# Projections of the next sample in two visits per slot in place of four, in an attention kernel between two expert layers

## The chip, the cores and the metric

The kernel runs on one core of a Trainium2 chip. The metric is device time in microseconds for one execution, from the median of several runs. TensorE multiplies matrices, VectorE reduces and combines, ScalarE evaluates exponentials and copies, GpSimd does masks and part of the rotary embedding, SyncE issues the DMAs. All of them run side by side and meet at semaphores.

## The reference, cut to what matters

Three layers follow one another on an input of 32 samples of 512 tokens and 256 features: an expert layer, attention with 16 heads of 16 features, and the expert layer again. The change is in the attention layer.

```python
x = x + 0.5 * ffn(layernorm(x))          # two experts of eight, chosen per sample
qkv = layernorm(x) @ Wqkv.T              # 512 x 768 for each sample
q, k = rotate(q), rotate(k)              # rotary embedding
attn = softmax(causal(q @ k.T / 4))      # 16 heads, 512 x 512
x = x + (attn @ v) @ Wo.T
x = x + 0.5 * ffn(layernorm(x))
```

## The kernel before

Each layer is a phase of its own. The attention phase (`attention_phase`) goes through the samples in slots: four slots (g = 0 to 3) to a sample, and each slot handles four heads. The work of one sample is spread over several samples' slots. In a slot for group G (sample s, part g) TensorE does, step by step for n = 0 to 10, the maxima scores of group G (`max_scores`, L882 to L906), which VectorE reduces to row maxima (L750), and the transposed scores of group G - 2 (`scores`, L908 to L926), on which ScalarE takes the exponential (L817). Scores have two PSUM banks, so step c waits for the exponential c - 2 (L914). Maxima scores have three banks, and a step waits for the reduction that last used its bank (L889). The two use opposite halves of TensorE's rows. Steps 0 to 3 have one score matmul of 512 columns, 4 to 7 two of 384 and 128, 8 and 9 two of 256.

Other work of TensorE is put between the steps by hand, in `slot` (L1017 to L1049):
- `turn_maxima` (L879) at n = 1 transposes the maxima of group G - 1. It waits for all eleven reductions of that group.
- `probs_v` (L941) at n = 2 and n = 8 multiplies exponentials with V.
- `turn_output` (L988) at n = 5 transposes the output of group G - 3. It waits for ScalarE's copy of it (L847), which ScalarE does after exponential 3.
- `project_qk` (L956) and `project_v` (L968) project the next sample, s + 1: in g = 0 and 1 two of the four 128-row blocks of Q and K in each slot, in g = 2 the four blocks of V. A block of Q or K is six matmuls of 512 columns, three for each half of the 256 features; a block of V is six matmuls of 256 columns. They use all of TensorE's rows. VectorE takes Q and K from PSUM (`begin_rope`, L724 and L725) behind its reductions 2 and 6, and ScalarE takes V (L864) behind exponentials 4 and 7.
- in g = 3, the transposes of sample s + 2 and the output projection of sample s - 1 (L980, L1002, L1011).

TensorE runs its matmuls in the order of the program. VectorE in g = 1 also has the low parts of rotated Q (`rope_low`, L731), and in g = 2 the layernorm statistics of sample s + 2 (L99 to L111) behind reduction 1. ScalarE copies the high parts of rotated Q and K (L823) in g = 1 and 2.

For the last sample there is no next one, so its slots have no projections. The first slots of the phase have projections but no scores yet.

Of the kernel before, what the change touches and what calls it, by code (L numbers as in the profile page):

```python
# [54 lines left out]
def wait(eng, sem, value):  # L55

    if isinstance(value, int) and value <= 0:
        return
    eng.wait_ge(sem, value)
# [441 lines left out]
def attention_phase(nc, tab, src, dst, cos, sin):  # L501
# [10 lines left out]
    with ExitStack() as ctx:  # L512
# [64 lines left out]
        def group(G):  # L577
            return not isinstance(G, int) or 0 <= G < B * 4

        def sample(s):  # L580
            return not isinstance(s.b, int) or 0 <= s.b < B
# [289 lines left out]
        def _(pe):  # L871
            def part(t, p):
                return t.hi if p == "hi" else t.lo

            def turn_maxima(s, g):

                G = 4 * s.b + g
                pe.wait_ge(max_done, 11 * G)
                nc.tensor.transpose(mx_ps[TURN_BANK][0:NT * GH, 0:P], mx[(g - 1) % 2][:].rearrange("p a i -> p (a i)"),  # L879
                                    tab.ident[:]).then_inc(mt_done, 1)  # L880

            def max_scores(s, g, n):  # L882

                G = 4 * s.b + g

                if n == 4:
                    wait(pe, mt_copied, G)
                else:
                    wait(pe, max_done, 11 * G + (-2, -1, 1, 2, None, 3, 4, 5, 6, 7, 8)[n])  # L889
                if n == 0:  # L890
                    pe.wait_ge(q_stacked, 96 * (s.b + 1))
                    pe.wait_ge(k_stacked, 96 * (s.b + 1))
                bank = mx_ps[MX_BANK[n]]
                i, heads = (3, [n]) if n < 4 else (2, [n - 4]) if n < 8 else (1, [2 * n - 16, 2 * n - 15]) if n < 10 else (0, range(4))
                w, nh = (i + 1) * P, len(heads)
                half, j = half_of(g)
                rows, const = slice(HP * half, HP * half + TERMS_ROWS), slice(HP * half, HP * half + HP)
                for at, a in enumerate(heads):
                    nc.tensor.matmul(bank[:, at * w:at * w + w], q_stack[s.par][rows, j + a, i * P:(i + 1) * P],  # L899
                                     k_stack[s.par][rows, j + a, 0:w], start=(at == 0), stop=False)  # L900

                last = bank[:, 0:nh * w].rearrange("p (a n) -> p a n", a=nh)[:, :, i * P:w]
                over = tab.mask[const, :].rearrange("p (a n) -> p a n", a=1)
                nc.tensor.matmul(last, tab.turn[const, HP:3 * HP], over.broadcast_to([HP, nh, P]), start=False, stop=False)  # L904
                nc.tensor.matmul(last[:, :, HP:P], tab.turn[const, 0:P], over[:, :, 0:HP].broadcast_to([HP, nh, HP]),  # L905
                                 start=False, stop=True).then_inc(mx_done, 1)  # L906

            def scores(s, g, c):  # L908

                G = 4 * s.b + g - 2  # L910
                ss, sg = of_group(s, g, 2)
                bank = st_ps[c % 2]

                wait(pe, exp_done, 10 * G + c - 1)  # L914
                if c == 0:
                    pe.wait_ge(rows_set[g % 2], 16 * (2 * s.b + (g - 2) // 2 + 1))
                a = c % 4 if c < 8 else 2 * (c - 8)
                half, j = half_of(sg)
                rows = slice(HP * half, HP * half + TERMS_ROWS + 1)

                work = [(a, 0, 0, 0)] if c < 4 else [(a, 1, P, 0), (a, 3, 3 * P, 3 * P)] if c < 8 else \
                    [(a, 2, 2 * P, 0), (a + 1, 2, 2 * P, 2 * P)]
                for ha, kt, q0, col in work:
                    ins = nc.tensor.matmul(bank[:, col:col + T - q0], k_stack[ss.par][rows, j + ha, kt * P:(kt + 1) * P],  # L924
                                           q_stack[ss.par][rows, j + ha, q0:T], start=True, stop=True)
                ins.then_inc(st_done, 1)  # L926

            def probs_v(s, g, lag, nth, kt):

                G = 4 * s.b + g - lag  # L930
                ss, sg = of_group(s, g, lag)
                if kt == 0:

                    wait(pe, on_done, G)
                    pe.wait_ge(v_copied, 2 * (ss.b + 1))
                pe.wait_ge(exp_done, 10 * G + (4, 8, 10, 8)[kt])
                pe.wait_ge(masked, 4 * G + nth + 1)
                for a in range(GH):
                    p = (probs[:, a, :], probs[:, 4 + a, 0:3 * P], probs[:, 8 + a // 2, (a % 2) * 2 * P:(a % 2) * 2 * P + 2 * P],
                         probs[:, 4 + a, 3 * P:])[kt]  # L940
                    ins = nc.tensor.matmul(pv_ps[32 * a:32 * a + 32, kt * P:T], v[ss.par][:, kt, head_of(sg, a), :], p,  # L941
                                           start=(kt == 0), stop=(nth == 3), tile_position=(0, 32 * a))
                ins.then_inc(pv_done, 1)

            def project_qk(n, t, half):

                idx = 4 * n.b + t
                if t == 0 and not half:
                    pe.wait_ge(xT_lo, NC * (n.b + 1))
                if t < 2 and not half:  # L950

                    wait(pe, res_done, 2 * (n.b - 2) - 1 + t)
                if t >= 2 and not half:
                    pe.wait_ge(rope_in, idx - 1)
                for i, (wp, xp) in enumerate(TERMS):
                    ins = nc.tensor.matmul(x_ps[t % 2][:], part(tab.qkv, wp)[:, int(half), t * P:(t + 1) * P],  # L956
                                           part(xT, xp)[:, int(half), :], start=(i == 0 and not half), stop=(i == 2 and half))
                if half:
                    ins.then_inc(qk_done, 1)

            def project_v(n, t):

                if t % 2 == 0:
                    pe.wait_ge(rope_in, 4 * (n.b + 1) - 1 + t // 2)
                i = 0
                for c in range(NC):
                    for xp, wp in TERMS:
                        ins = nc.tensor.matmul(x_ps[t // 2][:, (t % 2) * D:(t % 2) * D + D], part(xT, xp)[:, c, t * P:(t + 1) * P],  # L968
                                               part(tab.qkv, wp)[:, c, 2 * D:3 * D], start=(i == 0), stop=(i == 3 * NC - 1))
                        i += 1  # L970
                if t % 2:
                    ins.then_inc(v_done, 1)
# [44 lines left out]
            def slot(s, g):  # L1017
                G = 4 * s.b + g
                cur, run = group(G), group(G - 2)
                if isinstance(G, int) and G == 0:  # L1020
                    pe.wait_ge(stacks_set, 64)
                before = group(G - 3)
                for n in range(11):
                    if run and n < 10:
                        scores(s, g, n)
                    if cur:
                        max_scores(s, g, n)
                    if n == 2 and before:
                        probs_v(s, g, 3, 1, 1)
                    if n == 1 and group(G - 1):  # L1030
                        turn_maxima(s, g)
                    if n == 2 and before:
                        probs_v(s, g, 3, 2, 3)
                        probs_v(s, g, 3, 3, 2)
                    if n == 5 and before:
                        turn_output(s, g)
                    if g < 2 and sample(s + 1) and n in (0, 1, 4, 5):
                        project_qk(s + 1, 2 * g + (n > 3), half=(n in (1, 5)))
                    if g == 2 and sample(s + 1) and n in (0, 1, 4, 5):
                        project_v(s + 1, (0, 1, 4, 5).index(n))  # L1040
                    if g == 3 and sample(s + 2) and n == 0:
                        transposes(s + 2)
                    if run and n == 8:
                        probs_v(s, g, 2, 0, 0)
                    if g == 3 and sample(s + -1) and n == 4:
                        transpose_o(s + -1, s)
                    if g == 3 and sample(s + -1) and n >= 9:
                        project_o(s + -1, 2 * (n - 9))
                        project_o(s + -1, 2 * (n - 9) + 1)  # L1049

            schedule(pe, slot)


# [57 lines left out]
```

## Time and profile before

| | |
|---|---|
| median of 3 runs | 2402.93 us (2398.98 to 2409.86) |
| profiled execution | 2401.97 us |
| its span in the trace | 2400.2 us |
| matmuls busy | 2190.0 us (91%) |
| weight loads busy | 1279.8 us (53%) |
| VectorE busy | 1956.3 us (82%) |
| ScalarE busy | 1357.7 us (57%) |
| GpSimd busy | 1280.2 us (53%) |
| granted TensorE clock, mean | 0.979 |

The attention phase takes from about 440 to 2000 us of the span. In the timeline a row has the start, the duration, the engine, the line, the operation with output and inputs, and in brackets the idle time of the engine before it with who released it. "PE" is TensorE's matmuls and "PEld" its weight loads. Matmuls overlap one another in the rows, since each is shown until its result has landed: the pitch from start to start is what it costs in a stream.

### The profile page before, as it was taken

To read this page: it belongs to the slowest core of one execution; us is meant where nothing else is said; L and a number is where in the kernel's file an instruction comes from. 1 tells how busy PE (TensorE), PEld (TensorE's weight loads), DVE (VectorE), ACT (ScalarE), POOL (GpSimd) and SP (SyncE) were. 2 spreads that over 40 slices of the span, in tenths; PEclk is the share of its full clock that TensorE was granted. 3 is DMA by queue.
4 is the path that set the end of the run, shared out by engine and by line. 5 is a ranking of instruction groups with operands and counts; after the bars stand their busy time and mean duration, and the time that the engine had idled before them with its cause. 6 is when DMAs were issued, how large, how long until landed. Compare 5 with 4: busy or idle time off the path is not lost. (4 is left out here: it accounts for less than half of the span.)

```text
span 2400.2 us, 56572 instructions
## 1 busy us (share of the span) xinstructions
PE 2190.0 (91%) x19596; PEld 1279.8 (53%) x19596; DVE 1956.3 (82%) x4345; ACT 1357.7 (57%) x2567; POOL 1280.2 (53%) x1458
## 2 busy tenths in 40 slices
PE   2999999399999999999999999999999986999999
PEld 1666666245554555555455455545545543666666
DVE  4777777379989989998998999899899864777776
ACT  2455545046666666666666666666666663455454
POOL 3666666335545544554554555455455424666664
PEclk9999999779999999999999999999999997999999
DMA  5566665323444444344344434444433513665664
GB/s 162 172 203 204 203 204 191 88 63 89 97 89 93 95 92 90 89 99 89 93 95 89 90 90 99 89 96 94 86 90 92 93 39 111 187 210 193 208 205 164
DMA packets 280284, 295.50 MB, mean 123 GB/s; under 512 B 45664, under 2 KB 263104, under 8 KB 280000
## 3 DMA queue, kind: packets, MB, share of 16 engines
q1 hardware_dynamic: 279456, 290.83, 46.8%
q8 instruction: 157, 2.57, 0.5%
q14 instruction: 127, 1.04, 0.2%
q10 hardware_dynamic: 544, 1.05, 0.1%
HBM read 140.08 MB, written 83.89 MB: 93 GB/s over the span
## 5 line engine op out<-in xcount | busy, mean ns | idle before, releaser
L817 ACT ACTIVATE at_probs<-at_st_ps 128x512 f32<-128x512 f32 x1280 | 748.2, 604 | 508.6 <-PE at_st_ps L924 499.1
L750 DVE TENSOR_REDUCE at_mx<-at_mx_ps 128x1 f32<-128x512 f32 (+3 forms) x1408 | 839.8, 634 | 141.3 <-PE at_mx_ps L905 139.6
L672 POOL TENSOR_SCALAR_AFFINE_SELECT at_probs<-at_probs 128x512 f32<-128x512 f32 x512 | 320.5, 639 | 710.6 <-ACT at_probs L817 710.6
L899 PE MATMUL at_mx_ps<-at_k_stack,at_q_stack 48*128 48x512 f16 (+3 forms) x2048 | 502.3, 303 | 20.7 <-DVE at_mx L750 10.7
L924 PE MATMUL at_st_ps<-at_q_stack,at_k_stack 49*128 49x512 f16 (+3 forms) x2048 | 459.5, 302 | 65.7 <-ACT at_probs L817 64.2
L428 ACT ACTIVATE f_h<-f_h_ps,f_b1s 128x512 f32<-128x512 f32 x256 | 176.0, 688 | 359.2 <-PE f_h_ps L470 347.7
L924 PEld LDWEIGHTS at_st_ps<-at_q_stack,at_k_stack 49*128 49x128 f16 x2048 | 135.8, 94 | 433.4 <-ACT at_probs L817 332.0
L904 PE MATMUL at_mx_ps<-mask,turn 64*128 64x128 bf16 (+2 forms) x1408 | 342.2, 243 | 0.0
L941 PE MATMUL at_pv_ps<-at_probs,at_v 128*32 128x512 f32 (+3 forms) x4096 | 331.4, 441 | 0.3 <-POOL at_probs L672 0.3
L905 PE MATMUL at_mx_ps<-mask,turn 64*128 64x64 bf16 (+2 forms) x1408 | 281.5, 200 | 0.0
L486 PE MATMUL f_y_ps<-f_w2hi,f_hlo 128*128 128x256 f16 x1024 | 279.1, 273 | 0.0
L486 PE MATMUL f_y_ps<-f_w2hi,f_hhi 128*128 128x256 f16 x1024 | 279.1, 273 | 0.0
L486 PE MATMUL f_y_ps<-f_w2lo,f_hhi 128*128 128x256 f16 x1024 | 279.1, 273 | 0.0
L470 PE MATMUL f_h_ps<-f_xThi,f_w1hi 128*128 128x512 f16 x512 | 198.0, 387 | 30.1 <-DVE f_xTlo L377 29.8
L99 DVE BATCH_NORM_STATS2 f_stats<-f_x 128x6 f32<-128x256 f32 x256 | 89.8, 413 | 144.1 <-DMA f_x<-after_attention 72.7
L470 PE MATMUL f_h_ps<-f_xThi,f_w1lo 128*128 128x512 f16 x512 | 197.4, 385 | 0.0
L470 PE MATMUL f_h_ps<-f_xTlo,f_w1hi 128*128 128x512 f16 x512 | 196.9, 385 | 0.0
L678 POOL TENSOR_TENSOR at_by_sin<-at_swapped,at_sin 128x512 f32<-128x512 f32 x128 | 175.2, 1369 | 35.2 <-DVE at_swapped L725 35.2
L682 POOL TENSOR_TENSOR at_rotated<-at_by_cos,at_by_sin 128x512 f32<-128x512 f32 x128 | 182.1, 1423 | 18.8
L386 DVE TENSOR_TENSOR f_hlo<-f_h,f_hhi 128x512 f16<-128x512 f32 x256 | 173.2, 733 | 20.1 <-ACT f_hhi L429 20.1
L337 POOL TENSOR_TENSOR f_res<-f_x,f_b2q 128x1024 f32<-128x1024 f32 x64 | 151.1, 2361 | 61.5 <-DMA after_ffn<-f_res 30.6
L899 PEld LDWEIGHTS at_mx_ps<-at_k_stack,at_q_stack 48*128 48x128 f16 x2048 | 154.7, 93 | 54.2 <-DVE at_mx L750 25.6
(118 smaller groups left out, 4240.0 us busy)
## 6 DMA issues: line engine op xcount, KB each, us to landing
at_q_stack<-qk_image SPq DMA_DIRECT2D x192, 128.0 KB, 4.3
at_k_stack<-qk_image SPq DMA_DIRECT2D x192, 128.0 KB, 4.4
f_x<-in_x SPq DMA_DIRECT2D x32, 512.0 KB, 5.6
f_w1hi<-w_hi SPq DMA_DIRECT2D x128, 128.0 KB, 2.3
f_w1lo<-w_lo SPq DMA_DIRECT2D x128, 128.0 KB, 2.1
f_b2s<-in_b SPq DMA_DIRECT2D x128, 128.0 KB, 3.7
f_w2hi<-w_hi SPq DMA_DIRECT2D x128, 128.0 KB, 4.2
f_w2lo<-w_lo SPq DMA_DIRECT2D x128, 128.0 KB, 4.2
```

Of the source, the lines that this page charges most:

```text
L428: nc.scalar.activation(h32[j][:], h_ps[j][:], ACT.Gelu, bias=bias).then_inc(gelu_done, 1)
L470: ins = nc.tensor.matmul(h_ps[j][:], w, v, start=(n == 0), stop=(n == 3 * NC - 1))
L486: ins = nc.tensor.matmul(y_ps[t // 2][:, t % 2, :], v, w, start=(n == 0), stop=(n == 11))
L672: nc.gpsimd.affine_select(out=ap, in_=ap, compare_op=ALU.is_ge, fill=0.0, base=0, pattern=[[0, d] for d in dims] + [[1, P]], channel_multi ...
L682: nc.gpsimd.tensor_tensor(rotated[t % 2][:], by_cos[t % 2][:], by_sin[t % 2][:], ALU.add).then_inc(rope_done, 1)
L750: nc.vector.tensor_reduce(o_ap, i_ap, AX_X, ALU.max).then_inc(max_done, 1)
L817: nc.scalar.activation(probs[:, c, :], st_ps[c % 2][:], ACT.Exp, scale=DH ** -0.5).then_inc(exp_done, 1)
L899: nc.tensor.matmul(bank[:, at * w:at * w + w], q_stack[s.par][rows, j + a, i * P:(i + 1) * P], k_stack[s.par][rows, j + a, 0:w], start=(at ...
L904: nc.tensor.matmul(last, tab.turn[const, HP:3 * HP], over.broadcast_to([HP, nh, P]), start=False, stop=False)
L905: nc.tensor.matmul(last[:, :, HP:P], tab.turn[const, 0:P], over[:, :, 0:HP].broadcast_to([HP, nh, HP]), start=False, stop=True).then_inc(m ...
L924: ins = nc.tensor.matmul(bank[:, col:col + T - q0], k_stack[ss.par][rows, j + ha, kt * P:(kt + 1) * P], q_stack[ss.par][rows, j + ha, q0:T ...
L941: ins = nc.tensor.matmul(pv_ps[32 * a:32 * a + 32, kt * P:T], v[ss.par][:, kt, head_of(sg, a), :], p, start=(kt == 0), stop=(nth == 3), ti ...
```

## The change

In slots g = 0 and 1, the first half of a block of Q or K ran behind step 0 and its second half behind step 1; the next block's halves ran behind steps 4 and 5. Now both halves run behind step 1, and both of the next behind step 5. In slot g = 2, the four blocks of V ran behind steps 0, 1, 4 and 5; now two run behind step 1 and two behind step 5. The matmuls, their operands and their waits stay as they are.

```diff
-                    if g < 2 and sample(s + 1) and n in (0, 1, 4, 5):
-                        project_qk(s + 1, 2 * g + (n > 3), half=(n in (1, 5)))
-                    if g == 2 and sample(s + 1) and n in (0, 1, 4, 5):
-                        project_v(s + 1, (0, 1, 4, 5).index(n))
+                    if g < 2 and sample(s + 1) and n in (1, 5):
+                        project_qk(s + 1, 2 * g + (n > 3), half=False)
+                        project_qk(s + 1, 2 * g + (n > 3), half=True)
+                    if g == 2 and sample(s + 1) and n in (1, 5):
+                        project_v(s + 1, 2 * (n > 3))
+                        project_v(s + 1, 2 * (n > 3) + 1)
```

## Rows read from the trace of the kernel before

**Rows 1.** Busy time by stretches, one sample: engines, granted clock, DMA share, GB/s.
```profile
core 0: us, PE busy (x) PEld busy (x) DVE busy (x) ACT busy (x) POOL busy (x), PEclk, DMA share, GB/s
1000.00:1046.60 46.60, 44.37 (x453) 23.76 (x452) 42.28 (x98) 30.25 (x61) 24.15 (x30) 1.00 0.40 92
```

**Rows 2.** Waits of TensorE, 480 to 1960 us: total, times, longest.
```profile
PE at_st_ps L924 <- ACT at_probs L817: 61.0, 129, 0.6
```

**Rows 3.** Timeline of TensorE, a slot g = 0 of a middle sample.
```profile
1180.93 0.39 PE L924 MATMUL at_st_ps<-at_q_stack,at_k_stack 49*128 49x512 f16 x1
...
1182.50 0.28 PE L879 MATMUL at_mx_ps<-ident,at_mx 128*16 128x128 f32 x1
1182.62 0.38 PE L956 MATMUL at_x_ps<-at_xThi,qkv_hi 128*128 128x512 f16 x1
1182.83 0.38 PE L956 MATMUL at_x_ps<-at_xThi,qkv_lo 128*128 128x512 f16 x1
...
1183.36 0.39 PE L924 MATMUL at_st_ps<-at_q_stack,at_k_stack 49*128 49x512 f16 x1
...
1185.20 0.39 PE L924 MATMUL at_st_ps<-at_q_stack,at_k_stack 49*128 49x512 f16 x1
...
1186.97 0.66 PE L988 MATMUL at_pv_ps<-ident,at_o 128*128 128x128 f32 x4
1187.46 0.38 PE L956 MATMUL at_x_ps<-at_xThi,qkv_hi 128*128 128x512 f16 x1
...
1188.21 0.33 PE L924 MATMUL at_st_ps<-at_q_stack,at_k_stack 49*128 49x384 f16 x1
...
1190.84 0.28 PE L924 MATMUL at_st_ps<-at_q_stack,at_k_stack 49*128 49x256 f16 x1
...
1191.24 0.33 PE L899 MATMUL at_mx_ps<-at_k_stack,at_q_stack 48*128 48x128 f16 x3
1191.36 0.39 PE L924 MATMUL at_st_ps<-at_q_stack,at_k_stack 49*128 49x512 f16 x1
```

**Rows 4.** Timeline, slot g = 0 of the last sample, without projections: TensorE, then ScalarE's copy.
```profile
1925.77 0.39 PE L924 MATMUL at_st_ps<-at_q_stack,at_k_stack 49*128 49x512 f16 x1
...
1926.48 0.28 PE L879 MATMUL at_mx_ps<-ident,at_mx 128*16 128x128 f32 x1
...
1928.87 0.39 PE L924 MATMUL at_st_ps<-at_q_stack,at_k_stack 49*128 49x512 f16 x1
...
1930.00 0.33 PE L924 MATMUL at_st_ps<-at_q_stack,at_k_stack 49*128 49x384 f16 x1 [0.41 <-ACT at_probs L817]
...
1930.49 0.66 PE L988 MATMUL at_pv_ps<-ident,at_o 128*128 128x128 f32 x4
...
1929.84 0.59 ACT L847 ACTIVATE at_o<-at_pv_ps 128x512 f32<-128x512 f32 x1
```

**Rows 5.** Timeline of VectorE and TensorE, slots g = 1 and 2 of the middle sample.
```profile
1191.45 1.28 DVE L750 TENSOR_REDUCE at_mx<-at_mx_ps 128x2 f32<-128x512 f32 x2
...
1201.68 0.28 PE L924 MATMUL at_st_ps<-at_q_stack,at_k_stack 49*128 49x256 f16 x1
...
1202.51 0.39 PE L899 MATMUL at_mx_ps<-at_k_stack,at_q_stack 48*128 48x128 f16 x4 [0.26 <-DVE at_mx L750]
...
1203.07 0.38 PE L924 MATMUL at_st_ps<-at_q_stack,at_k_stack 49*128 49x512 f16 x1
...
1203.57 1.27 DVE L750 TENSOR_REDUCE at_mx<-at_mx_ps 128x4 f32<-128x512 f32 x2
...
1208.17 0.68 DVE L750 TENSOR_REDUCE at_mx<-at_mx_ps 128x1 f32<-128x512 f32 x1
1208.91 0.33 PE L899 MATMUL at_mx_ps<-at_k_stack,at_q_stack 48*128 48x384 f16 x1
...
1210.50 0.33 PE L924 MATMUL at_st_ps<-at_q_stack,at_k_stack 49*128 49x384 f16 x1
```

**Rows 6.** Timeline of VectorE, the same subtraction in slots g = 1 and 2.
```profile
1193.25 1.25 DVE L731 TENSOR_TENSOR at_qk_lo<-at_rotated,at_qk_hi 128x512 f16<-128x512 f32 x1
...
1204.77 0.68 DVE L731 TENSOR_TENSOR at_qk_lo<-at_rotated,at_qk_hi 128x512 f16<-128x512 f32 x1
```

## The prediction, made before the changed kernel was built or run

> **What bounds the kernel now.** I read the busy shares first, then the waits of TensorE, and then one slot of four heads step by step in the timeline. The view by stretches says that in one sample of the attention phase (46.6 us, four slots) the matmul row is busy 44.37 us, VectorE 42.28, ScalarE 30.25, at a granted clock of 1.00, the 2.4 GHz level [rows 1]. That makes TensorE look full. The weight loads on the same engine are busy 23.76 us, about half. The Trainium skill ("Perfetto Trace Analysis", section "Identifying the Most-Contended Engine") says that the share of matmul busy time isn't a measure of how close TensorE is to its limit, since matmuls are pipelined, and points to the share of weight loads. These rows agree that 95% and 51% describe the same stretch.
>
> The waits show who holds TensorE up: between 480 and 1960 us the score matmuls (L924) wait for ScalarE's exponentials 129 times, 61.0 us together [rows 2]. So a slot is a chain in which TensorE and ScalarE take turns: step n+2 of the scores can't start before exponential n is done, since there are two score banks. What one more or one less matmul costs depends on where in this chain it stands. TensorE runs its matmuls in program order, so whatever stands behind a waiting score matmul waits too.
>
> The timeline of a slot g = 0 of a middle sample [rows 3] has its score steps 0, 2, 3, 6 and 9 at 1180.93, 1183.36, 1185.20, 1188.21 and 1190.84, and the next slot at 1191.36: 10.43 us. The best view is one that the kernel gives for free: in the last sample there is no next sample to project, and the same slot g = 0 runs without any projection [rows 4]. It shows what the chain does where the projection is not there to fill it. Its step 3 starts at 1928.87 and step 5 at 1930.00, which is 1.13 us later, held by the exponential of step 3 (the row says 0.41 us idle, released by ScalarE). Its transposes of the output (L988) start at 1930.49, 1.62 us after step 3, behind ScalarE's copy of the output, which ends at 1929.84 + 0.59 = 1930.43.
>
> **The change, part by part.** No matmul is added or taken away. In each slot with g = 0, 1 or 2, half of the first projection goes from step 0 to step 1, and half of the second from step 4 to step 5. The number of visits (a run of full-array matmuls between score steps) falls from four to two per slot.
>
> Unit costs. A visit of three L956 matmuls takes 0.74 us from its first matmul to the next score step (1182.62 to 1183.36) [rows 3], 0.75 after the output transposes (1187.46 to 1188.21). The pitch in it is 0.21 to 0.22 us (1182.62 to 1182.83), so three more matmuls add 0.65, and a visit of six takes 1.40. Six L968 matmuls have half the columns each; I take the same 0.65 for them.
>
> First visit, g = 0. Without projection, step 0 to the transpose of the maxima (L879) is 0.71 us (1925.77 to 1926.48) [rows 4]; from that to the projection 0.12 (1182.50 to 1182.62) [rows 3]. Then step 2 starts at 0.71 + 0.12 + 1.40 = 2.23 after step 0, against 2.43 now. Gain 0.20: that is what a change from half-array to full-array work and back costs, and it is real wherever nothing else is waited for. The Trainium skill ("TensorE: Matmul & The Clock Gate", section "LDWEIGHTS (loading the stationary operand)") gives the 128 columns of a weight load 107 ns; two of them left uncovered per visit would be 0.21, an estimate by that page; the 0.20 of the rows agrees.
>
> Second visit, g = 0. Now the half at step 4 lies in the time in which step 5 would wait for exponential 3. Taken away, step 5 waits: it starts 1.13 after step 3, the transposes of the output 1.62 after it (not 1.77 as now, 1185.20 to 1186.97), the projection 0.49 later (1186.97 to 1187.46), step 6 a further 1.40: 1.62 + 0.49 + 1.40 = 3.51 us, against 3.01 now (1185.20 to 1188.21). Loss 0.50. Behind step 6 nothing has slack: steps 7 and 8 wait for exponentials that follow step 6. So the slot g = 0 becomes 0.30 longer. Bounds for this part: if step 5 had no wait, the gain would be 0.20 again; if the wait hid nothing, the loss is the 0.65 of the three matmuls. I take 0.50, since both ends of it stand in [rows 4].
>
> Slot g = 1. Here the transpose of the maxima has to wait: VectorE ends the last reduction of the slot before at 1191.45 + 1.28 = 1192.73 [rows 5], 1.37 after the slot's start, while now the transpose comes at 1.99 and doesn't feel it. Moved up, it starts at about 1.43; then 0.12 + 1.40 gives step 2 at 2.95 against 2.84 now: loss 0.11 in place of the gain, because six matmuls now stand behind a wait that three of them used to fill. The second visit costs 0.50 again. Of the 0.61 a part is given back: the last maxima step waits for VectorE now. Step 9 at 1201.68 and last maxima matmul at 1202.51 are 0.83 apart (0.26 idle, released by L750), against 0.40 in g = 0 (1190.84 to 1191.24) [rows 3, 5]. VectorE's work in this slot is as before, so these 0.43 are slack for TensorE: 0.61 - 0.43 = 0.18 longer.
>
> Slot g = 2. VectorE's last reduction of g = 1 (1203.57, 0.68 for one) ends 1.18 after the slot's start now [rows 5], and 1.00 after it once the slot starts 0.18 later, so the transpose of the maxima starts at 1.06; + 0.12 + 1.40 = 2.58 for step 2. Now it is 2.48: loss 0.10. In the second visit the maxima of step 5 start at 1208.91, right when VectorE's reduction of step 2 is done (1208.17 + 0.68 = 1208.85), and that is behind the layernorm statistics, not behind TensorE. It stays where it is, at 5.84. All of the six V matmuls that stood before it now come behind it: 0.65 longer, with step 6 at 8.08 in place of 7.43 (1210.50 - 1203.07), and this includes the 0.10. Slot g = 3 has no projection and keeps its length.
>
> Sum: 0.30 + 0.18 + 0.65 = 1.13 us per sample. Projections run beside scores in the slots of 30 samples, and in one more only in g = 2: 30 x 1.13 + 0.65 = 34.6 us. The profiled execution took 2401.97 us (its span 2400.20 and 1.77 around it), 0.04% below the median of 2402.93. So 2402 + 34.6 gives 2437, which I leave as it is for the median.
>
> What is passed on the way costs nothing: the second half of each projection stays in its place in the order, so the vector engine's rotation, the V copies on ScalarE, GpSimd's products and the SyncE loads and stores behind them are released after the same matmul as before, only later by what step 2 and step 6 are late. The rotation of g = 1 could feel this first. Its cover is VectorE's own queue, which is without a gap in that slot.
>
> **The rivals.**
> A, TensorE is full, and only the switches count. Each visit removed saves 0.20, six per sample: 6 x 0.20 x 31 = 37 us less, 2366. For it speaks the 95% of [rows 1]. Against it stands that step 5 without the half before it waits 0.41 us in [rows 4]. The Trainium skill ("TensorE: Matmul & The Clock Gate", section "Loop structure matters more than you think") asks for matmuls back to back, and by that rule this change is a gain, though none by the clock, which is at 1.00 in [rows 1] already. Chance 0.07.
> B, the delay is swallowed in g = 1 and g = 2, since VectorE is busy 42.28 of 46.6 us and sets their length: then only the 0.30 of g = 0 is left, 30 x 0.30 = 9 us, 2411, not measurable against before. For it speaks the wait at 1202.51; against it that this wait holds only 0.43 and that g = 2 has no such wait at its end. It would need a slack of 0.65 there. Chance 0.13.
> C, the shift also brings VectorE and GpSimd over one another. The same subtraction (L731) takes 1.25 us at 1193.25 and 0.68 at 1204.77 [rows 6]; GpSimd is at work on the rotation beside the first. One more such overlap per sample on the chain of g = 1 costs up to 0.57 x 31 = 18 us: 2455. Chance 0.14.
> The forecast has 0.66.
>
> **How the numbers follow.** Likeliest 2437. Its own bounds are the first visit's 0.11 and 0.10 falling away (30 x 0.2 = 6 less) and the loss of the second at its full 0.65 in g = 0 and 1 (30 x 0.30 = 9 more): 2428 to 2447. The range must hold 8 in 10: forecast and C, up to 2456, and down to 2416, which leaves out A and most of B. A measurement of this kernel can tell about 0.5% (12 us) from no change. Faster by more: A, 0.07. Within: B, 0.13. Slower by more: 0.80.
>
> **What would show it.** In the profile after, in a middle sample: slots of about 10.7, 11.9, 11.2 and 13.9 us; step 2 of g = 0 at 2.23; score step 5 idle 0.4 us or so before it, released by ScalarE, in each of the three slots; waits of L924 for L817 grown by 90 cases or more; in g = 1 the transpose of the maxima released by VectorE, and no wait left before the last maxima step. If step 5 starts less than 1.13 us after step 3, the second visit is wrong; if step 6 in g = 2 is at 7.4, the third term is; if the reductions or L731 are longer than before, C has come.

## The result, and the profile after

The changed kernel takes 2442.86 us (median of 4 executions, 2438.85 to 2449.67), the kernel before 2404.89 us in the same comparison. The ratio is 1.0162, with a 95% interval of 1.0127 to 1.0197: slower by 38 us (31 to 47). The forecast was 2437, a loss of 34.6, in a range of 2416 to 2456.

The view by stretches, for one middle sample, as in [rows 1] (columns as there: engines with busy time and count, granted clock, DMA share, GB/s):

```profile
1197.67:1245.70 48.03, 44.35 (x454) 24.34 (x454) 42.79 (x97) 29.90 (x60) 24.09 (x29) 1.00 0.43 90
```

The sample takes 48.03 us in place of 46.6. The matmuls are busy 44.35 us as before (44.37 in [rows 1]), at the same granted clock. So all of the loss is time in which no matmul is in flight. The waits of TensorE between 480 and 2000 us show the releaser:

```profile
PE at_st_ps L924 <- ACT at_probs L817: 98.9, 221, 0.6
PE at_mx_ps L899 <- DVE at_mx L750: 4.7, 8, 1.4
```

The second row reads in the kernel before, between 480 and 1960 us:

```profile
PE at_mx_ps L899 <- DVE at_mx L750: 10.7, 33, 1.4
```

The score matmuls wait for exponentials 221 times in place of 129 (98.9 us in place of 61.0, [rows 2]): 92 waits more, in 90 or so slots that have both projections and scores. The waits of the maxima matmuls (L899) for VectorE fall from 33 to 8: the one before the last maxima step of g = 1 is gone in nearly every sample.

The timeline of a slot g = 0 answers to [rows 3]:

```profile
1197.67 0.39 PE L924 MATMUL at_st_ps<-at_q_stack,at_k_stack 49*128 49x512 f16 x1
1197.90 0.38 PE L924 MATMUL at_st_ps<-at_q_stack,at_k_stack 49*128 49x512 f16 x1
1198.39 0.28 PE L879 MATMUL at_mx_ps<-ident,at_mx 128*16 128x128 f32 x1
1198.50 0.38 PE L956 MATMUL at_x_ps<-at_xThi,qkv_hi 128*128 128x512 f16 x1
...
1199.89 0.39 PE L924 MATMUL at_st_ps<-at_q_stack,at_k_stack 49*128 49x512 f16 x1
1201.73 0.39 PE L924 MATMUL at_st_ps<-at_q_stack,at_k_stack 49*128 49x512 f16 x1
...
1202.87 0.33 PE L924 MATMUL at_st_ps<-at_q_stack,at_k_stack 49*128 49x384 f16 x1 [0.41 <-ACT at_probs L817]
...
1203.36 0.66 PE L988 MATMUL at_pv_ps<-ident,at_o 128*128 128x128 f32 x4
1203.85 0.38 PE L956 MATMUL at_x_ps<-at_xThi,qkv_hi 128*128 128x512 f16 x1
...
1205.24 0.33 PE L924 MATMUL at_st_ps<-at_q_stack,at_k_stack 49*128 49x384 f16 x1
...
1208.39 0.39 PE L924 MATMUL at_st_ps<-at_q_stack,at_k_stack 49*128 49x512 f16 x1
```

Step 1 now follows step 0 after 0.23 us, and step 2 comes at 2.22 (1199.89 - 1197.67), 0.21 earlier than before. Then step 5 stands 0.41 us for ScalarE, 1.14 behind step 3, and step 6 comes 3.51 behind step 3 (1205.24 - 1201.73) in place of 3.01. The row of step 5 in the last sample of the kernel before [rows 4] had the same 0.41. The same 0.41 stands before step 5 in g = 1 and g = 2.

The slots, each as the median distance between the first score matmuls of neighbouring slots over the middle samples. In one kernel nearly all of them repeat to some hundredths of a microsecond from sample to sample, which is far finer than the times themselves, so the experiments below are read by them:

| us | g = 0 | g = 1 | g = 2 | g = 3 | sum |
|---|---|---|---|---|---|
| before | 10.43 | 11.71 | 10.59 | 13.85 | 46.58 |
| forecast for after | 10.73 | 11.89 | 11.24 | 13.85 | 47.7 |
| after | 10.72 | 11.87 | 11.58 | 13.85 | 48.02 |

Thirty samples at 1.44, and one more g = 2 at 0.99, are 44 us. The spans differ by 42.3 (2442.5 and 2400.2), and the medians by 38. Single executions of one kernel differ by some us. A part of that is the start of the phase: the first score matmul stands at 506.09 in the profiled execution before and at 501.83 in the one after.

### The profile page after: what moved, and what is told of

Read it like the earlier page. It is cut to its first block and busy times, and to the rows that moved or that the text cites. A ratio compares the mean times of both kernels' runs of the same rounds, so it can differ in the third digit from the quotient of the medians.

```text
span 2442.5 us, 56572 instructions
## 1 busy us (share of the span) xinstructions
PE 2190.0 (90%) x19596; PEld 1297.0 (53%) x19596; DVE 1970.9 (81%) x4345; ACT 1347.9 (55%) x2567; POOL 1277.9 (52%) x1458
## 3 DMA queue, kind: packets, MB, share of 16 engines
q1 hardware_dynamic: 279456, 290.83, 46.6%
## 5 line engine op out<-in xcount | busy, mean ns | idle before, releaser
L924 PE MATMUL at_st_ps<-at_q_stack,at_k_stack 49*128 49x512 f16 (+3 forms) x2048 | 450.0, 302 | 102.6 <-ACT at_probs L817 101.4
L899 PE MATMUL at_mx_ps<-at_k_stack,at_q_stack 48*128 48x512 f16 (+3 forms) x2048 | 498.0, 302 | 18.4 <-DMA at_k_stack<-qk_image 10.4
L899 PEld LDWEIGHTS at_mx_ps<-at_k_stack,at_q_stack 48*128 48x128 f16 x2048 | 155.4, 93 | 59.8 <-DVE at_mx L750 27.9
```

## The experiments

**1. Each visit by itself.** The first visit merged, and the second as before:

```diff
-                    if g < 2 and sample(s + 1) and n in (0, 1, 4, 5):
+                    if g < 2 and sample(s + 1) and n in (1, 4, 5):
+                        if n == 1:
+                            project_qk(s + 1, 2 * g, half=False)
                         project_qk(s + 1, 2 * g + (n > 3), half=(n in (1, 5)))
-                    if g == 2 and sample(s + 1) and n in (0, 1, 4, 5):
+                    if g == 2 and sample(s + 1) and n in (1, 4, 5):
+                        if n == 1:
+                            project_v(s + 1, 0)
                         project_v(s + 1, (0, 1, 4, 5).index(n))
```

> Only the first visit is merged (behind step 1); the second stays at steps 4 and 5. Theory T (TensorE's chain, with the exponential of step 3 as the thing the second visit used to hide): g = 0 shorter by 0.20 us (10.23), g = 1 unchanged, since its delay of 0.10 behind the transpose of the maxima is taken by the wait of the last maxima step for VectorE (11.70), g = 2 longer by about 0.18 (10.77), because the transpose of the maxima waits for VectorE until about 1.24 after the slot's start. Sum about 0 per sample: the same time as before, within 3 us. Rival A (switches cost, nothing waits): 0.20 less in each of three slots, 19 us faster than before. Rival M (merging as such is what costs, in either place): about half of the 38 us, some 19 us slower.

Measured: ratio to before 0.9984 (0.9968 to 0.9999), 2398.77 us against 2403.80. Slots 10.22, 11.79, 10.77, 13.85, sum 46.63. Theory T holds in g = 0 (10.23 expected) and g = 2 (10.77); g = 1 is 0.09 longer than expected. The wait that was to take the delay is there, with the same 0.26 us idle as in [rows 5]:

```profile
1200.57 0.40 PE L899 MATMUL at_mx_ps<-at_k_stack,at_q_stack 48*128 48x128 f16 x4 [0.26 <-DVE at_mx L750]
```

It ends later, since VectorE's own queue in g = 1 is longer. VectorE has a second subtraction L731 there, behind reduction 3. It took 1.03 us in the kernel before, and takes 1.12 here, where GpSimd's mask comes later against the slot. In the kernel before:

```profile
1197.44 1.03 DVE L731 TENSOR_TENSOR at_qk_lo<-at_rotated,at_qk_hi 128x512 f16<-128x512 f32 x1
1197.30 0.64 POOL L672 TENSOR_SCALAR_AFFINE_SELECT at_probs<-at_probs 128x512 f32<-128x512 f32 x1 [1.66 <-ACT at_probs L817]
```

In this one:

```profile
1195.42 1.12 DVE L731 TENSOR_TENSOR at_qk_lo<-at_rotated,at_qk_hi 128x512 f16<-128x512 f32 x1
1195.36 0.63 POOL L672 TENSOR_SCALAR_AFFINE_SELECT at_probs<-at_probs 128x512 f32<-128x512 f32 x1 [1.75 <-ACT at_probs L817]
```

Against the slot's start (1191.36 and 1189.34) the mask begins at 5.94 and 6.02, and in both kernels L731 ends 0.53 to 0.55 after it.

Neither A (19 us faster) nor M (19 slower) is borne out. The first visit saves 0.21 where nothing is waited for, and gives it back in g = 1 and 2. The median is 5 us lower all the same, which the slots (0.05 more per sample) don't explain. The executions of this kernel had a mean granted clock of 0.977 to 0.983, all but two of the kernel before 0.974 to 0.977, and the one of those at 0.983 took 2391.76 us. So a few microseconds between medians are no reading of the slots; where in the program they arise was not followed.

The second visit merged, and the first as before:

```diff
-                    if g < 2 and sample(s + 1) and n in (0, 1, 4, 5):
+                    if g < 2 and sample(s + 1) and n in (0, 1, 5):
+                        if n == 5:
+                            project_qk(s + 1, 2 * g + 1, half=False)
                         project_qk(s + 1, 2 * g + (n > 3), half=(n in (1, 5)))
-                    if g == 2 and sample(s + 1) and n in (0, 1, 4, 5):
+                    if g == 2 and sample(s + 1) and n in (0, 1, 5):
+                        if n == 5:
+                            project_v(s + 1, 2)
                         project_v(s + 1, (0, 1, 4, 5).index(n))
```

> Only the second visit is merged (behind step 5); the first stays at steps 0 and 1. Theory T: g = 0 longer by 0.50 us (10.93), g = 1 by 0.07 (11.77, the rest taken by the wait for VectorE), g = 2 by 0.65. If in g = 2 GpSimd's product again slides over VectorE's subtraction L731 (as it does in the changed kernel, where it takes 1.08 us in place of 0.68), g = 2 is longer by 0.99 in all (11.58). Sum 1.2 without and 1.56 with that overlap: 37 or 47 us slower than before, so at least the whole loss of the change. Rival A: 19 us faster. Rival M: about 19 us slower.

Measured: 1.0184 (1.0144 to 1.0223), 2444.43 us. Slots 10.93, 11.78, 11.58, 13.85, sum 48.13: the expected 10.93, 11.77 and 11.58. Of these the 11.58 is no forecast, since its overlap of VectorE and GpSimd was read from the changed kernel, which had run by then. TensorE in g = 0:

```profile
1203.28 0.39 PE L924 MATMUL at_st_ps<-at_q_stack,at_k_stack 49*128 49x512 f16 x1
...
1204.41 0.33 PE L924 MATMUL at_st_ps<-at_q_stack,at_k_stack 49*128 49x384 f16 x1 [0.41 <-ACT at_probs L817]
...
1204.90 0.66 PE L988 MATMUL at_pv_ps<-ident,at_o 128*128 128x128 f32 x4
1205.39 0.38 PE L956 MATMUL at_x_ps<-at_xThi,qkv_hi 128*128 128x512 f16 x1
...
1206.78 0.33 PE L924 MATMUL at_st_ps<-at_q_stack,at_k_stack 49*128 49x384 f16 x1
```

Step 5 waits 0.41 us, and step 6 is 3.50 behind step 3. The second visit alone brings the whole loss.

**2. Is it the number of visits, or the place?** Two visits, but the second one behind step 4, where the exponential is waited for:

```diff
-                    if g < 2 and sample(s + 1) and n in (1, 5):
+                    if g < 2 and sample(s + 1) and n in (1, 4):
...
-                    if g == 2 and sample(s + 1) and n in (1, 5):
+                    if g == 2 and sample(s + 1) and n in (1, 4):
```

> Two visits per slot as in the change, but the second behind step 4 in place of step 5: all six matmuls lie in the time in which step 5 would wait for exponential 3. Theory T taken on TensorE alone: step 3 to step 6 takes 3.00 us in place of 3.51, g = 0 is 10.22, and the kernel is 40 us or so faster than the changed one and within 8 us of before. Theory T with VectorE's queue: the output transposes come 0.64 later behind step 3 than before, VectorE's normalisation with them, and its reduction 6 in g = 0 starts 0.4 us later; since VectorE has no gap from there to the end of g = 1, the last maxima step of g = 1 waits longer and g = 1 grows by up to 0.6: 10 to 20 us slower than before, still 20 to 30 faster than the changed kernel. Rival M (two visits are worse than four wherever they stand): as slow as the changed kernel, 38 us slower than before.

Measured: 1.0044 (1.0029 to 1.0058), 2415.42 us. Slots 10.50, 11.88, 10.77, 13.85, sum 47.00. Seven tenths of the loss per sample are gone (0.42 in place of 1.44), so rival M falls: with the same two visits it is the place that counts. The kernel stays 12 us slower than before, where the version of the theory with VectorE's queue had 10 to 20. Step 3 to step 6 is 3.01 us, as expected:

```profile
1187.84 0.39 PE L924 MATMUL at_st_ps<-at_q_stack,at_k_stack 49*128 49x512 f16 x1
...
1189.90 0.33 PE L924 MATMUL at_st_ps<-at_q_stack,at_k_stack 49*128 49x384 f16 x1
...
1190.26 0.66 PE L988 MATMUL at_pv_ps<-ident,at_o 128*128 128x128 f32 x4
...
1190.85 0.33 PE L924 MATMUL at_st_ps<-at_q_stack,at_k_stack 49*128 49x384 f16 x1
```

The version of the theory with TensorE alone falls too. The output transposes come 2.42 behind step 3, and VectorE's queue is late with them. VectorE in this kernel, in the same slot:

```profile
1190.38 0.56 DVE L750 TENSOR_REDUCE at_mx<-at_mx_ps 128x1 f32<-128x384 f32 x1 [0.87 <-PE at_mx_ps L905]
1190.95 0.26 DVE L762 RECIPROCAL at_inverse<-at_pv_ps 128x16 f32<-128x16 f32 x1
1191.31 0.62 DVE L767 TENSOR_TENSOR at_on<-at_pv_ps,at_inverse 128x64 f32<-128x64 f32 x4
1191.85 0.55 DVE L750 TENSOR_REDUCE at_mx<-at_mx_ps 128x1 f32<-128x384 f32 x1
```

It stands idle 0.87 us ahead of reduction 5, and reduction 6 comes 1.00 after step 6 (1191.85 - 1190.85). In the kernel before it comes 0.47 after step 6, which stands at 1188.21 [rows 3]:

```profile
1188.68 0.56 DVE L750 TENSOR_REDUCE at_mx<-at_mx_ps 128x1 f32<-128x384 f32 x1
```

From there VectorE has no gap. The last maxima step feels it, and already in g = 0: it stands 0.68 behind step 9 (1194.15 and 1193.47), where it stood 0.40 behind it before, so the slot is 10.50 and not 10.22. I had expected the wait in g = 1 alone. There it shows at the transpose of the maxima, which starts 1.66 after the slot's start (1195.94 - 1194.28).

**3. The transpose of the maxima.** The changed kernel, with this transpose behind the first projection:

```diff
-                    if n == 1 and group(G - 1):
-                        turn_maxima(s, g)
...
                         project_v(s + 1, 2 * (n > 3) + 1)
+                    if n == 1 and group(G - 1):
+                        turn_maxima(s, g)
```

> The changed kernel, with the transpose of the maxima behind the first projection of the slot in place of ahead of it. If in g = 1 the six matmuls stand idle behind its wait for VectorE (it starts 1.43 after the slot's start), they now start at about 1.25, step 2 comes at 2.76 in place of 2.94, and g = 1 shrinks from 11.87 to 11.69. In g = 2 step 2 comes 0.2 earlier, but the slot keeps its 11.58, since the maxima of step 5 wait for VectorE's reduction 2. Sum -0.18 per sample, 5 us faster than the changed kernel. If that wait doesn't matter, nothing changes; if the wait is what costs in g = 2 as well, 11 us.

Measured: 2435.94 us, 1.0129 to before (1.0091 to 1.0167). Slots 10.73, 11.68, 11.58, 13.85. g = 1 is 11.68 where 11.69 was expected, and g = 2 keeps its 11.58. The times themselves can't tell this kernel from the changed one (1.0127 to 1.0197); the slots can. In the changed kernel the transpose in g = 1 starts at 1209.83, 1.44 after the slot's start at 1208.39, and the six matmuls behind it:

```profile
1209.83 0.28 PE L879 MATMUL at_mx_ps<-ident,at_mx 128*16 128x128 f32 x1
1209.94 0.38 PE L956 MATMUL at_x_ps<-at_xThi,qkv_hi 128*128 128x512 f16 x1
```

So the second term of the forecast, 0.11 lost behind this wait in place of a gain, is as described.

**4. What the forecast missed in g = 2.** There the slot grew by 0.99 in place of 0.65. In the trace after, TensorE, GpSimd and VectorE in g = 2, which starts at 1220.26:

```profile
1221.15 1.28 POOL L678 TENSOR_TENSOR at_by_sin<-at_swapped,at_sin 128x512 f32<-128x512 f32 x1
...
1221.89 1.08 DVE L731 TENSOR_TENSOR at_qk_lo<-at_rotated,at_qk_hi 128x512 f16<-128x512 f32 x1
...
1225.70 0.68 DVE L750 TENSOR_REDUCE at_mx<-at_mx_ps 128x1 f32<-128x512 f32 x1
...
1226.44 0.33 PE L899 MATMUL at_mx_ps<-at_k_stack,at_q_stack 48*128 48x384 f16 x1
...
1228.69 0.33 PE L924 MATMUL at_st_ps<-at_q_stack,at_k_stack 49*128 49x384 f16 x1
```

L731 in this slot makes the low parts of K, as in g = 1 those of Q: VectorE has the subtraction in both slots, behind reductions 0 and 3. The first one takes 1.08 us, and ends 0.54 after GpSimd's product (1222.97 and 1222.43). In the kernel before it took 0.68 here [rows 6], for the product had ended at 1203.53 + 1.27 = 1204.80, when L731 began:

```profile
1203.53 1.27 POOL L678 TENSOR_TENSOR at_by_sin<-at_swapped,at_sin 128x512 f32<-128x512 f32 x1
```

The maxima of step 5 start right behind reduction 2 as before, at 6.18 in place of 5.84. TensorE had been ready for step 5's maxima before that, in spite of the wait for the exponential, which was over at 5.67 (1225.93 - 1220.26):

```profile
1225.93 0.39 PE L924 MATMUL at_st_ps<-at_q_stack,at_k_stack 49*128 49x384 f16 x2 [0.41 <-ACT at_probs L817]
```

To see whether this is the cause, both kernels were run with GpSimd's two operations cut to 64 of 512 columns for the block in question. The rotation of that block is left out but for these columns, so the times stand for less work on GpSimd:

```diff
+                w = P // 2 if t == 3 else T
-                nc.gpsimd.tensor_tensor(by_sin[t % 2][:], swapped[t % 2][:], sin_t[:], ALU.mult).then_inc(sin_done, 1)
+                nc.gpsimd.tensor_tensor(by_sin[t % 2][:, 0:w], swapped[t % 2][:, 0:w], sin_t[:, 0:w], ALU.mult).then_inc(sin_done, 1)
...
-                nc.gpsimd.tensor_tensor(rotated[t % 2][:], by_cos[t % 2][:], by_sin[t % 2][:], ALU.add).then_inc(rope_done, 1)
+                nc.gpsimd.tensor_tensor(rotated[t % 2][:, 0:w], by_cos[t % 2][:, 0:w], by_sin[t % 2][:, 0:w], ALU.add).then_inc(rope_done, 1)
```

> The changed kernel with GpSimd's two rotation operations (L678, L682) on 64 of 512 columns for the last of the four Q and K blocks of a sample (t = 3), the block whose products run early in g = 2. Part of K's rotation is left out by this. Theory C' (VectorE's subtraction L731 in g = 2 can't run while GpSimd's product does, and this overlap is the part of the loss in g = 2 that the prediction missed): L731 takes 0.68 in place of 1.08, the reduction 2 ends near 5.8 in place of 6.13, and g = 2 is 11.24 in place of 11.58; sum 0.34 less per sample, 10 us. Rival: the extra 0.34 has another cause (the V copies, the transpose of the maxima); then g = 2 stays at 11.58.

> The same shortened rotation operations of GpSimd in the kernel before, as the control. Theory C': there the product ended at 1.73, just as L731 began at 1.70, so nothing is gained: g = 2 stays at 10.59 and the slots sum to 46.58. Against the shortened changed kernel the loss of the change is then 0.29 + 0.17 + 0.65 = 1.11 per sample, which is the predicted 1.13. Rival: if GpSimd costs time in g = 2 in the kernel before as well, g = 2 shrinks here too.

Measured: the changed kernel 2433.20 us (one execution), slots 10.72, 11.87, 11.21, 13.85; the kernel before 2401.11 us (one execution), slots 10.43, 11.71, 10.59, 13.85. The shortened changed kernel (lines one lower):

```profile
1218.59 0.32 POOL L679 TENSOR_TENSOR at_by_sin<-at_swapped,at_sin 128x64 f32<-128x64 f32 x1
...
1219.33 0.69 DVE L732 TENSOR_TENSOR at_qk_lo<-at_rotated,at_qk_hi 128x512 f16<-128x512 f32 x1
```

The product starts no earlier, but is over at 1218.91, and the subtraction takes 0.69. g = 2 is 0.37 shorter, and the control keeps its length. Step 6 of g = 2 now starts 8.06 after the slot's start (1225.76 - 1217.70), where the forecast, which had left out the overlap, said 8.08. Between the two shortened kernels the slots sum to 47.65 and 46.58: a loss of 1.07 per sample, close to the forecast's 1.13. Both of GpSimd's operations were shortened together; that it is the product which meets L731 is read from the rows. The two executions of this pair are too few for the times themselves to say more.

**5. The same overlap, turned into a gain.** If L731 can't run beside the product, VectorE may as well do its next reduction meanwhile. In g = 1 L731 took 1.25 us [rows 6]. The first visit merged as in the first experiment, the transpose of the maxima behind it, and

```diff
-                    if g in (1, 2) and sample(s + 1) and n in (0, 3):
+                    if g in (1, 2) and sample(s + 1) and n in (2 - g, 3):
                         rope_low(s + 1, 2 * (g - 1) + (n == 3))
```

> The kernel of the first merged visit, with the transpose of the maxima behind that visit, and in g = 1 VectorE's first subtraction L731 behind its reduction 1 in place of 0. In g = 1 L731 waits now for GpSimd's product to end (1.89 to 3.14, the product to 2.59). Theory C': VectorE does reduction 1 in that time, L731 gets in at about 2.59, VectorE's queue in g = 1 is some 0.5 shorter, the last maxima step waits no more and g = 1 is 11.3 in place of 11.7. g = 0 is 10.22. In g = 2 the product of GpSimd may come 0.3 later against the slot and L731 with it: 10.6 to 10.85. Sum 0.4 to 0.6 less per sample than before, 2385 to 2391 us. Rival: GpSimd's second operation starts before L731 gets in, L731 waits until 4.3, and g = 1 is longer than 11.7 by about 0.6.

Measured: 0.9953 (0.9937 to 0.9970), 2390.12 us. Slots 10.23, 11.19, 10.93, 13.85. In g = 1 L731 takes 0.68 (1187.58, with the product ended at 1186.42 + 1.27 = 1187.69); the slot is 0.52 shorter than before. g = 2 is 10.93 where 10.6 to 10.85 was expected. There L731 takes 1.09, for the same reason as in the changed kernel: against the start of the slot, GpSimd's product comes later.

Then in g = 2 the same order (`n in (1, 3)` in both slots):

> As the kernel with L731 behind reduction 1 in g = 1, and the same in g = 2. There L731 stood from 1.62 to 2.71 and GpSimd's product to 2.17. Theory C': VectorE does reduction 1 meanwhile and L731 gets in at 2.2 for 0.68 us; the statistics and reduction 2 behind it end at about 5.7 in place of 6.12, the maxima of step 5 start then, and g = 2 is 10.5 in place of 10.93. Sum 45.8 per sample in place of 46.2: 13 us less, 2377 us. Rival: GpSimd's next operation (2.32) gets in first and L731 waits until 3.8; g = 2 is then 11.5 or more.

Measured: 0.9881 (0.9862 to 0.9899), 2373.12 us against 2403.16. Slots 10.23, 11.19, 10.41, 13.85, sum 45.69. This is the best of all, faster than both kernels. The two engines in g = 2:

```profile
1187.59 1.27 POOL L678 TENSOR_TENSOR at_by_sin<-at_swapped,at_sin 128x512 f32<-128x512 f32 x1
1189.00 1.63 POOL L682 TENSOR_TENSOR at_rotated<-at_by_cos,at_by_sin 128x512 f32<-128x512 f32 x1
...
1188.80 0.68 DVE L731 TENSOR_TENSOR at_qk_lo<-at_rotated,at_qk_hi 128x512 f16<-128x512 f32 x1
```

The subtraction gets in as the product ends, at 1188.86, and GpSimd's next operation is the one that waits: 1.63 us, where it takes 1.54 in the changed kernel and 1.27 at best.

How much of it is the new order of VectorE and how much the merged first visit? The kernel before with `n in (2 - g, 3)` alone:

> The kernel before, with only VectorE's L731 behind reduction 1 in place of 0, in g = 1 (g = 2 keeps its order). Here the first visit is split as before, so the maxima of step 1 end at 2.06 and reduction 1 takes 2.1 to 2.8, while GpSimd's product ends at 2.59 and its next operation starts at 2.74. Theory C' (whichever of the two holds the port keeps the other out): L731 gets to its turn at about 2.7, a hair before or after GpSimd's second operation. If before, it ends at 3.3 to 3.4, VectorE's queue is 0.4 shorter, and g = 1 goes from 11.71 to 11.3: 12 us faster than before. If after, L731 ends near 4.8 and g = 1 is 12.5 or more: 20 us or so slower. If the order of reduction and subtraction doesn't matter (rival: the gain of the merged kernels came from the merged visit), g = 1 stays at 11.71.

Measured: 0.9975 (0.9961 to 0.9989), 2398.14 us. Slots 10.43, 11.28, 10.93, 13.85, sum 46.49. L731 gets in at 1192.74, and GpSimd's next operation starts at 1192.78 and takes 1.79:

```profile
1192.74 0.68 DVE L731 TENSOR_TENSOR at_qk_lo<-at_rotated,at_qk_hi 128x512 f16<-128x512 f32 x1
```

So g = 1 gains 0.43 by the order alone, where 0.4 was expected, and the rival falls. The gain is mostly lost in g = 2, where L731 takes 1.09 now; the forecast of 12 us had not followed the shift that far. The new order in both slots without the merged visit was not run, so how the 30 us of the best kernel divide between the two is known for g = 0 and 1 alone: the merged visit gives 0.20 in g = 0 and, with the transpose behind it, 0.09 in g = 1 (11.28 and 11.19).

**6. The wait of step 8.** Every slot also stands at step 8 for an exponential. The kernel with 2390.12 us, with the fourth block of V behind step 7:

```diff
-                    if g == 2 and sample(s + 1) and n in (1, 4, 5):
+                    if g == 2 and sample(s + 1) and n in (1, 4, 7):
...
-                        project_v(s + 1, (0, 1, 4, 5).index(n))
+                        project_v(s + 1, (0, 1, 4, 7).index(n))
...
-                    if g == 2 and sample(s + 1) and n in (4, 7):
+                    if g == 2 and sample(s + 1) and n in (5, 7):
                         v_copy(s + 1, int(n == 7))
```

> The kernel of the run before, and in g = 2 the fourth block of V goes from step 5 to step 7, where step 8 waits for an exponential (0.46 us idle at each slot's step 8); ScalarE's first V copy goes behind exponential 5. Theory T (a projection is free where TensorE would wait for an exponential): step 5 to step 6 loses 0.65, step 6 to step 8 gains 0.27, so g = 2 is 0.3 to 0.4 shorter than in the run before, 10 to 12 us. Rival: VectorE's queue sets g = 2, and nothing is gained.

Measured: 0.9954 (0.9941 to 0.9968), 2392.19 us; g = 2 is 10.97, where it was 10.93. The rival holds. Step 7's scores start at 1203.30, but its maxima only at 1203.80: VectorE's reduction 4 ends then, and frees their bank.

```profile
1203.30 0.32 PE L924 MATMUL at_st_ps<-at_q_stack,at_k_stack 49*128 49x384 f16 x1
...
1203.80 0.33 PE L899 MATMUL at_mx_ps<-at_k_stack,at_q_stack 48*128 48x384 f16 x1
```

## Why the prediction was right, and where it was off

- First visit, g = 0: step 2 at 2.23 forecast, 2.22 measured. The 0.20 for one visit less is right, and it is all that rival A had. Experiment 1 shows it alone (10.43 to 10.22). What in the switch takes this time is not shown by any run.
- Second visit, g = 0: 3.51 from step 3 to step 6 forecast, 3.51 measured, and the slot 10.72 for 10.73. What made this possible was the last sample of the kernel before [rows 4]: it held the wait that the change would uncover.
- g = 1: +0.18 forecast, +0.16 measured. Step 9 comes 0.59 later against the slot's start (10.91 and 10.32), of which the slack took 0.43. The wait behind the transpose of the maxima is real (experiment 3). The wait for VectorE before the last maxima step swallowed the rest, as forecast from [rows 5].
- g = 2: +0.65 forecast, +0.99 measured. This is the term that was mis-sized. The prediction said of the maxima of step 5, which wait for reduction 2, "It stays where it is, at 5.84", and that is what failed: they started at 6.18. Reduction 2 is behind the statistics, these are behind reduction 1, and this one is behind L731, which met GpSimd. Rival C had the mechanism and the price of one overlap, but put it in g = 1 and made it an alternative; it came in g = 2, beside the forecast, and cost 0.34 (0.99 - 0.65) where its price was up to 0.57. The reason for the shift is in the sum itself. In g = 1 the last scores come 0.59 later in a slot that grows by 0.16 only, so the last exponential, GpSimd's mask behind it, and the product behind the mask come 0.43 later against g = 2 (0.89 and 0.46 after its start). The loss at the first visit of g = 2 was also larger than forecast, step 2 at 2.69 in place of 2.58, but it cost nothing, since reduction 2 ended later still (experiment 3: the slot keeps its 11.58 without it).
- In all: 1.44 per sample in place of 1.13; 44 us by the slots against a forecast of 34.6 in the whole. The measured 38 lies between, and within its interval it can't tell the two apart. That the medians come nearer to the forecast than the slots do is luck.
- The bounds around the likeliest value were not what their own terms give: the 6 us less make 2431, not 2428, and the 0.10 of g = 2 could not fall away, as the 0.65 held it already.
- That the profiled execution starts its scores 4.3 us earlier than that of before isn't explained by the change: in the shortened kernel with the order of before they start at 501.47 too. What it does come from was not tried.
- Rival A (0.07) is refuted by a kernel that is slower by 1.3% at least, by the 92 waits more and by experiment 1, where the one merged visit with the 0.20 to gain leaves the sum of the slots as it was. Rival B (0.13) is refuted by g = 2.
- The rule of matmuls back to back, which the prediction set beside rival A, is about keeping the clock up: the Trainium skill ("TensorE: Matmul & The Clock Gate", section "Loop structure matters more than you think") says that it is the loop nest which decides whether matmuls stay warm. The granted clock was 1.00 in both samples, so there was nothing to win by it here, and no gain of another kind follows from it. In this kernel the matmuls that stood between the score steps were what kept TensorE back to back.

## What to carry to other kernels

Independent work on the engine that alternates with another is worth most where that engine would wait; moving it to the next gap, even by one step and with fewer switches, adds both the wait and the work to the chain. Look for a stretch where the filler is missing already (here the last sample): its rows show the wait that a change will uncover. And follow a shift of one engine through every queue that hangs on it, as two engines that can't work side by side may come over one another a slot later.

## What the runs showed of the hardware

- VectorE's subtraction of two SBUF tensors and GpSimd's operations hardly run side by side. Alone, L731 takes 0.68 us. It took 1.25 in g = 1 of the kernel before, 1.08 in g = 2 of the changed one, and each time it ended 0.54 to 0.55 after GpSimd's product. The second one in g = 1 took 1.03, and ended 0.53 after GpSimd's mask (1198.47 and 1197.94). In g = 1 of the kernel before that product is

```profile
1192.68 1.27 POOL L678 TENSOR_TENSOR at_by_sin<-at_swapped,at_sin 128x512 f32<-128x512 f32 x1
```

  which ends at 1193.95, with L731 at 1193.25 + 1.25 = 1194.50 [rows 6]. The reductions from PSUM keep their 0.68: the one at 1192.65 ran beside this product. Where L731 comes first, GpSimd's operation is the longer one (1.79 in experiment 5). The Trainium skill ("SBUF — State Buffer", section "Who interferes with whom") says that a VectorE instruction with two SBUF inputs contends with a GpSimd instruction that reads SBUF, and that the order of issue decides who is blocked. The traces agree, in both orders.
- One visit of full-array matmuls between half-array score steps costs 0.20 us more when it is split in two (step 2 at 2.22 us with one visit ahead of it, 2.43 with two). What takes the time is not shown.
- Score and maxima matmuls on opposite halves start within 0.01 us of each other in step 0 (1197.67 and 1197.68). Without a visit between them the scores of step 1, behind 512 columns, follow after 0.23 us (1197.90), and the maxima, behind 704 columns, after 0.32 (1197.99).
